# Dividing the attention output with channels on partitions, and four steps in another place

## The reference

```
x = x + attention(layernorm(x)) @ Wo.T       # 16 heads of 8 channels, 64-token window over
                                             # the token's block and the block before
n = layernorm(x)
scores = sigmoid(n @ gate_kernel) + gate_bias
comb   = the 4 best experts of the 2 best groups of 4, weights normalised, times 2.5
x = x + sum_e comb[e] * (silu(n @ w_gate[e]) * (n @ w_up[e])) @ w_down[e]      # 16 experts of 64
      + (silu(n @ sw_gate) * (n @ sw_up)) @ sw_down                            # shared, 128 wide
```

## Time and profile before

| | before |
|---|---|
| median of 3 runs (lowest to highest) | 708.99 us (707.56 to 709.0) |
| the profiled execution: time, span | 710.96 us, 709.2 us |
| mean granted clock of TensorE, of full speed | 0.984 |
| busy PE, PEld | 662.5 us (93%), 521.9 us (74%) |
| busy DVE, ACT, POOL | 590.6 (83%), 530.9 (75%), 478.5 us (67%) |

### The profile page before, as it was taken

How to read it: one execution, slowest core, us unless ns; L and a number is a source line. 1 busy time by engine, 2 the same in 40 slices (tenths; PEclk the granted TensorE clock), 3 DMA queues, 4 the chain that set the end, 5 groups by cost and what they waited for, 6 DMA issues and landing times.

```text
span 709.2 us, 20018 instructions
## 1 busy us (share of the span) xinstructions
PE 662.5 (93%) x6488; PEld 521.9 (74%) x6488; DVE 590.6 (83%) x1708; ACT 530.9 (75%) x1635; POOL 478.5 (67%) x599
## 2 busy tenths in 40 slices
PE   3988889999999999999999999999999999989996
PEld 2767657777787877778787877778787877767775
DVE  2777797989989898988989898998989898888663
ACT  3775869787887879787887879787887879763432
POOL 3503157878788787877778687877878686776523
PEclk9998899999999999999999999999999999999999
DMA  6000022040414123040413113040313213041321
GB/s 174 20 13 31 1 73 96 17 141 28 130 50 120 59 74 105 19 131 30 122 58 116 63 63 117 12 137 30 120 59 105 74 56 110 6 134 35 117 76 46
DMA packets 50245, 52.60 MB, mean 74 GB/s; under 512 B 5664, under 2 KB 31904, under 8 KB 50080
## 3 DMA queue, kind: packets, MB, share of 16 engines
q1 hardware_dynamic: 50208, 52.14, 23.7%
HBM read 43.20 MB, written 4.72 MB: 68 GB/s over the span
## 4 chain that ended last, share of the span: by engine, by line
PE 30%; ACT 28%; DVE 19%; issue 12%; POOL 8%; DMA 1%; DVEq 1%; POOLq 0%; ACTq 0%; SPq 0%
ACT probs L603 12%; DVE neg_max L778 6%; PE PS L1057 5%; PE PS L903 4%; ACT q_by_head L554 4%; PE PS L865 4%; PE PS L867 4%; PE PS L866 4%; ACT v_bd L554 3%; ACT th L570 3%; DVE tu L767 3%; DVE probsT L738 3%; POOL hh L482 2%; POOL X L539 2%; POOL X L533 2%
## 5 line engine op out<-in xcount | busy, mean ns | idle before, releaser
L603 ACT ACTIVATE probs<-PS,neg_max 128x96 f32<-128x96 f32 (+1 forms) x1024 | 247.8, 351 | 75.7 <-DVE neg_max L778 75.7
L477 POOL TENSOR_TENSOR gate<-gate,spread 128x512 f32<-128x512 f32 x124 | 158.7, 1280 | 105.5 <-ACT gate L554 53.1
L482 POOL TENSOR_TENSOR hh<-gate,tu 128x512 f32<-128x512 f32 x108 | 139.3, 1290 | 14.7 <-DVE tu L767 7.3
L1057 PE MATMUL PS<-wd,hh 128*128 128x128 f32 x1024 | 137.5, 277 | 7.7 <-DVE OUT L793 2.9
L1057 PEld LDWEIGHTS PS<-wd,hh 128*128 128x128 f32 x1024 | 126.8, 192 | 20.7 <-DVE OUT L793 9.8
L778 DVE TENSOR_REDUCE neg_max<-PS 128x4 f32<-128x384 f32 (+1 forms) x256 | 122.1, 516 | 13.4 <-PE PS L903 11.7
L767 DVE SCALAR_TENSOR_TENSOR tu<-th,PS 128x512 f32<-128x512 f32 x128 | 87.5, 684 | 51.3 <-ACT th L570 39.5
L865 PE MATMUL PS<-x_hi,w_hi 128*128 128x512 f32 x288 | 125.0, 434 | 0.0
L570 ACT ACTIVATE th<-PS 128x512 f32<-128x512 f32 x128 | 80.5, 629 | 50.9 <-PE PS L867 49.3
L738 DVE STREAM_TRANSPOSE probsT<-probs 128x768 f32<-128x768 f32 (+1 forms) x128 | 114.4, 894 | 0.0
L867 PE MATMUL PS<-x_lo,w_hi 128*128 128x512 f32 x288 | 114.2, 397 | 0.0
(11 more groups left out here) (108 smaller groups left out, 986.9 us busy)
## 6 DMA issues: line engine op xcount, KB each, us to landing
spread<-weights_by_expert SPq DMA_DIRECT2D x248, 128.0 KB, 3.0
X<-x SPq DMA_DIRECT2D x32, 256.0 KB, 3.4
OUT<-H SPq DMA_DIRECT2D x16, 256.0 KB, 3.0
out<-OUT SPq DMA_DIRECT2D x16, 256.0 KB, 3.0
ffn_stage<-w_gu SPq DMA_DIRECT2D x1, 1152.0 KB, 7.0
wd<-w_down SPq DMA_DIRECT2D x1, 512.0 KB, 6.8
weights_by_expert<-cT SPq DMA_DIRECT2D x16, 32.0 KB, 1.6
probsT<-w_att SPq DMA_DIRECT2D x1, 192.0 KB, 3.1
```

What stands on the lines that cost most here:

```text
L477: tt(gate2[:, :], gate[:, k % 2, :], spread[:, k % SP_BUFS, :], ALU.mult).then_inc(s_g2, 1)
L482: tt(hh[:, k % 2, :], gate2[:, :], tu[:, k % 2, :], ALU.mult).then_inc(s_h, 1)
L603: ins = nc.scalar.activation(probs[:, u % PROB_BUFS, tt, 2 * rows + e, j0:KW], PS[:, rows, n * KW + j0:n * KW + KW], ACT.Exp, bias=neg_max ...
L1057: ins = mm(PS[:, 7, r], hh[:, k % 2, r], wd[:, k, :], start=(k == 0 and n == 0), stop=(k == NP - 1), skip_group_check=True)
```

## The change

The division keeps channels on partitions. DVE takes the reciprocal of the 128x32 sums before turning them. POOL multiplies the turned reciprocals by a mask, so that `by_block` (128 x 256) holds for each of eight query blocks only the lanes of that block (`EXPAND`, stages 14 and 17, steps 6 and 1). At `OT` PE multiplies a constant 0/1 map `to_channel` with it in one f32 matmul, which puts each token's reciprocal on the partitions of its channels, and DVE multiplies `o_f` with the result into `oT`. `ON`, its transposes and ACT's copy to `oT` are gone. The next values matmuls wait for DVE's product in place of ACT's copy. The two maps are made once, by DVE and POOL.

Four things move: DVE's addition to `OUT` from the middle of step 5 to the end of step 4 (stage 36; SP's store goes with it); the shared expert's matmuls on PE ahead of the values matmuls of step 1, and `fa` on DVE ahead of the turning; the statistics of the first norm ahead of the turning in step 3; and the extra matmuls also run in steps 0 to 3 of slot 3 (`warming`).

```diff
-OT, ON, OW = 14, 15, 16
+EXPAND = (14, 17)
+OT, OW = 14, 16
...
-YE = 37
+YE = 36
...
-    (POST, (OT, OT + 4, ON, ON + 4, OW, OW + 4, SH)), (WEIGHTS, (CT,)))
+    (POST, (OT, OT + 4, OW, OW + 4, SH)), (WEIGHTS, (CT,)))
...
+def warming(slot, s):
+
+    return filling(slot) or slot.fixed and slot.n == 3 and s < FF % STEPS
...
-        o_rs = sb("o_rs", [P, 8, 4])
-        o_n = sb("o_n", [P, 2, P])
+        lane_of = sb("lane_of", [P, 4])
+        block_of = sb("block_of", [P, NQ])
+        to_channel = sb("to_channel", [P, P])
+        by_block = sb("by_block", [P, GB, NQ, Q])
...
-        sums_of = ident.rearrange("p (v h c a) -> p c h a v", v=4, h=2, c=4)
...
+                    for b, stage in enumerate(EXPAND):
+                        g, _ = at(sl, s, stage)
+                        if g:
+                            if not (g.fixed and g.n == 0):
+                                taken(pool, slot_before(sl), (OT + 4 * b) % STEPS, POST)
+                            pool.wait_ge(s_sum_t, g.n * GB + b + 1)
+                            whole = [P, NQ, Q]
+                            tt(by_block[:, b, :, :], sums_t[:, b, :].unsqueeze(1).broadcast_to(whole),
+                               block_of[:, :].unsqueeze(2).broadcast_to(whole), ALU.mult).then_inc(s_exp, 1)
                     if sl.fixed and sl.n == 0 and s == LN1 + 1:
                         pool.wait_ge(s_w, 16 * LOADS)
+                        pool.wait_ge(s_lane, 1)
+                        for a in range(4):
+                            shape = [P, 4, D]
+                            ins = tt(to_channel[:, 32 * a:32 * a + 32].rearrange("p (v d) -> p v d", d=D),
+                                     lane_of[:, a:a + 1].unsqueeze(2).broadcast_to(shape),
+                                     grouprow.unsqueeze(2).broadcast_to(shape), ALU.mult)
+                        ins.then_inc(s_chan, 1)
...
-                    g, b = at(sl, s, ON, 4, GB)
-                    if g:
-                        side, bank = filled(act, sl, s, POST)
-                        copy(oT[:, :], bank[:, 0:T]).then_inc(s_taken[side], 1)
...
+                        v_.tensor_reduce(block_of[:, :], ident.rearrange("p (v t a) -> p t v a", t=NQ, a=HG),
+                                         mybir.AxisListType.XY, ALU.add)
+                        v_.tensor_reduce(lane_of[:, :], ident.rearrange("p (x a) -> p a x", a=HG),
+                                         AX_X, ALU.add).then_inc(s_lane, 1)
...
                             if u % 4 == 3:
                                 dve.wait_ge(s_sum, g.n * NU + u + 1)
+                                link(sl, v_.reciprocal(sums[:, b, :], sums[:, b, :]))
                                 v_.transpose(sums_t[:, b, :], sums[:, b, :]).then_inc(s_sum_t, 1)
...
-                    g, _ = at(sl, s, YE)
-                    if g:
-                        dve.wait_ge(s_dn, g.n + 1)
-                        dve.wait_ge(s_cp[g.par], turn(g))
-                        v_.tensor_tensor(OUT[:, g.par, :, :], tiles(PS[:, 7, :]), OUT[:, g.par, :, :],
-                                         ALU.add).then_inc(s_y, 1)
                     if s == (RT + 1) % STEPS:
                         for place in range(2, 6):
                             routing(sl, s, place)
...
-                        link(sl, v_.reciprocal(o_rs[:, :, :], bank[:, T:T + Q].rearrange("p (a v) -> p a v", v=4)))
-                        v_.tensor_tensor(o_n[:, :, :].rearrange("p n (a v d) -> p (n a) v d", v=4, d=D),
-                                         bank[:, 0:T].rearrange("p (a v d) -> p a v d", v=4, d=D),
-                                         o_rs[:, :, :].unsqueeze(3).broadcast_to([P, 8, 4, D]),
-                                         ALU.mult).then_inc(s_taken[side], 1)
+                        dve.wait_ge(s_o, g.n * GB + b + 1)
+                        v_.tensor_tensor(oT[:, :], o_f[:, :], bank[:, 0:T], ALU.mult).then_inc(s_taken[side], 1)
...
-                    turn_probs()
+                    g, _ = at(sl, s, SH)
+                    if g:
+                        side, bank = filled(dve, sl, s, POST)
+                        dve.wait_ge(s_ths, g.n + 1)
+                        v_.scalar_tensor_tensor(fa[:, :], th_s[:, :], 1.0, bank, ALU.add, ALU.mult
+                                                ).then_inc(s_taken[side], 1)
                     g = first_norm(sl, s)
                     if g:
                         dve.wait_ge(s_x[g.par], turn(g))
                         stats(sl, X[:, g.par, :, :], NT, st1, mv1).then_inc(s_mv1, 1)
+                    turn_probs()
...
-                    g, _ = at(sl, s, SH)
-                    if g:
-                        side, bank = filled(dve, sl, s, POST)
-                        dve.wait_ge(s_ths, g.n + 1)
-                        v_.scalar_tensor_tensor(fa[:, :], th_s[:, :], 1.0, bank, ALU.add, ALU.mult
-                                                ).then_inc(s_taken[side], 1)
                     sum_probs()
+                    g, _ = at(sl, s, YE)
+                    if g:
+                        dve.wait_ge(s_dn, g.n + 1)
+                        dve.wait_ge(s_cp[g.par], turn(g))
+                        v_.tensor_tensor(OUT[:, g.par, :, :], tiles(PS[:, 7, :]), OUT[:, g.par, :, :],
+                                         ALU.add).then_inc(s_y, 1)
                     g, _ = at(sl, s, XT)
...
-                    if filling(sl) and at(sl, s, SC, 1, NU)[0]:
+                    if warming(sl, s) and at(sl, s, SC, 1, NU)[0]:
                         for _ in range(BUSY):
                             mm(PS[:, 7, 0:WV], w_hi[:, WQ:WQ + P], w_hi[:, WQ:WV], start=True, stop=True)
...
+                    g, _ = at(sl, s, SH)
+                    if g:
+                        x2 = x2_hi[:, g.par, :], x2_lo[:, g.par, :]
+                        pe.wait_ge(s_x2l, g.n * GB + GB)
+                        for place, n in ((POST, WG), (LATE, WU)):
+                            side, bank = free(place)
+                            exact3(bank, *w2(n + P * NP), *x2).then_inc(s_filled[side], 1)
+
...
                         if not later and not (g.fixed and g.n == 0 and b == 0):
-                            pe.wait_ge(s_o, g.n * GB + b)
+                            taken(pe, slot_before(sl) if b else sl, (OT if b else OT + 4) % STEPS, POST)
...
                         side, bank = free(POST)
-                        pe.wait_ge(s_o, g.n * GB + b + 1)
-                        for half in range(2):
-                            nc.tensor.transpose(bank[:, P * half:P * half + P], o_f[:, P * half:P * half + P], ident)
-                        pe.wait_ge(s_sum_t, g.n * GB + b + 1)
-                        for c in range(4):
-                            ins = mm(PS[32 * c:32 * c + 32, RING[side], T:T + Q], sums_t[:, b, :], sums_of[:, c, :, :, :],
-                                     start=True, stop=True)
-                        ins.then_inc(s_filled[side], 1)
-                    g, b = at(sl, s, ON, 4, GB)
+                        if g.fixed and g.n == 0:
+                            pe.wait_ge(s_chan, 1)
+                        pe.wait_ge(s_exp, g.n * GB + b + 1)
+                        mm(bank[:, 0:T], to_channel[:, :], by_block[:, b, :, :].rearrange("p t q -> p (t q)"),
+                           start=True, stop=True).then_inc(s_filled[side], 1)
+                    g, b = at(sl, s, OW, 4, GB)
                     if g:
                         side, bank = free(POST)
-                        taken(pe, sl, (s - 1) % STEPS, POST)
-                        for half in range(2):
-                            ins = nc.tensor.transpose(bank[:, P * half:P * half + P], o_n[:, half, :], ident)
-                        ins.then_inc(s_filled[side], 1)
-                    g, b = at(sl, s, OW, 4, GB)
-                    if g:
-                        side, bank = free(POST)
-                        taken(pe, slot_before(sl) if s == 0 else sl, (s - 1) % STEPS, POST)
+                        taken(pe, sl if b else slot_before(sl), (OT + 4 * b) % STEPS, POST)
                         if g.fixed and g.n == 0 and b == 0:
                             pe.wait_ge(s_wf, 16 * FFN_LOADS)
                         for half in range(2):
                             r = slice(P * half, P * half + P)
                             ins = mm(bank[:, r], oT[:, r], wo[:, :], start=True, stop=True)
                         ins.then_inc(s_filled[side], 1)
-                    g, _ = at(sl, s, SH)
-                    if g:
-                        x2 = x2_hi[:, g.par, :], x2_lo[:, g.par, :]
-                        pe.wait_ge(s_x2l, g.n * GB + GB)
-                        for place, n in ((POST, WG), (LATE, WU)):
-                            side, bank = free(place)
-                            exact3(bank, *w2(n + P * NP), *x2).then_inc(s_filled[side], 1)
-
```

(15 more changed lines are left out.)

## The result

| | before, same chip | after |
|---|---|---|
| median of 4 runs (lowest to highest) | 709.0 us (707.56 to 710.1) | 754.27 us (752.87 to 755.91) |
| ratio, with its 95% interval | 1 | 1.0632 [1.0604, 1.0661] |
| profiled execution: time, span | 710.96, 709.2 us | 752.87, 751.1 us |

The forecast was 687 us (679 to 698). The kernel became slower by 45.3 us, far outside the range and past the slower rival too (716).

A forecast was written before the change was run, and what follows sets the result against it. PE was taken to bound the slot; 1.4 us saved a slot, 16.8 over twelve, 20.9 with the other slots and drain, plus 1.6 for the fill, made 22.5 us off: 687 us forecast (679 to 698).

The forecast's parts named there:

- the slower rival: POOL's product releases PE in both halves and holds up PE and POOL work behind it; 716 us, chance 0.05.
- rival (3): The slower rival: POOL's product at 2.0 us loses 0.9 us a slot; 716 us, chance 0.05.
- The new wait for POOL's product: Step 6, PE at the new matmul: a new standstill of 0.4 us a slot, 0.3 in the sum.
- `ON`'s transposes: Two transposes of o_n per half group leave PE, saving 0.27 us each half, in steps 3 and 7.
- rival (1): ACT and DVE replace PE as the bound; the slot gains only 0.9 us; 696 us, chance 0.20.
- The shared products between scores and values: Shared products precede the values matmuls, which stand 1.4 us later; claimed free, as ACT copies o_f only afterwards.
- X: Step 4, PE's wait for POOL's normalisation: earlier statistics remove it, 0.45 us a slot.
- OUT: Step 5, PE's wait for DVE before the down products: the earlier addition removes it, 0.34 us a slot.
- fa: Step 2, PE's wait for DVE: fa ahead of the turning removes it, 0.27 us a slot.
- The matmul in place of the transposes: One f32 matmul of 256 columns per half, 0.46 us, replaces o_f transposes and spreading passes of 0.60 us.
- DVE's and ACT's chain: About as long as PE's from step 5 to 1; 0.2 us a slot taken off for DVE's longer chain and margin.
- The fill: Slot 3's warming matmuls keep PE's clock at 1.0: 1.6 us gained, best case 3.

The follow-up runs named there:

- after +19: The changed kernel with 19 more idle instructions (repeats of an already met wait) ahead of PE's first matmul; 699.6 us, ratio 0.9823 against before.
- the moves alone: The changed kernel with the old division and no warming in slot 3, leaving the moves of OUT, shared products with fa, and statistics; 702.27 us, ratio 0.9873.
- the late matmul: The changed kernel with 19 more instructions, the new matmul behind its step's down products and DVE's oT product at the step's end; 694.8 us, ratio 0.9763.
- the division alone: The changed kernel with 19 more instructions and the three moves undone, leaving new division and warming; 707.67 us, ratio 0.9973.

## Why the prediction was wrong

**The step that failed** is one that the prediction never took, a term of the sum put at nothing without a reason: it priced removed and added instructions by their time on the engine and let the place of PE's loop in its instructions be what it was. The unrolled slots 0 to 3 became 57 instructions shorter, the transposes and the spreading passes weighing more than the warming that was added; the loop slid from seven pieces into eight. That costs five times a standstill of 6.2 us and 2.9 us of half clock behind it, 45.5 us together; with 19 idle instructions the profiled execution is 53.3 us shorter (699.57 against 752.87). Of that, 50 are the five turns (89.0 against 39.5 twice, 10 us each: the 9.1 above and some 0.9 of work out of step behind them) and 3.3 the fill, which ended at 114.61 us in the one and 111.36 in the other: the clock was 0.50 from 64 to 68 us in the one and 1.00 in the other, a fall that comes and goes between executions, and I have one trace of each. No row that I cited could show the jump; the row of the instruction queue, 20 packets, and the loop's edges in the program, both within some 0.2 of a piece of a border (offset included), would have raised the question. The rivals had the right sign once, for another reason: POOL's product takes 0.62 us, not the 2.0 that rival (3) needed.

**The rest of the sum** (the row after +19): the slot gained 0.56 us by medians (0.50 over the whole loop) where 1.4 was forecast, and the kernel 12.6 us where 22.5 was. By the two profiled executions, 11.4 us apart, 5.9 came in the loop where 16.8 was forecast, 4.1 up to slot 4 where 3.4 was, and 1.4 behind the loop where 2.3 was.
- The new wait for POOL's product, taken at 0.4 us (0.3 in the sum), is 1.0 to 1.3 in the twelve slots, 1.13 at the median, and 19.1 us over 15 times. Step 6 is 0.88 longer than forecast. The product was sized rightly (0.62 us). That POOL would come 0.66 us earlier was not, since a transfer took part of the gain (0.33), nor that PE would come 0.79 earlier (1.10, mostly by the larger gain at X). This is the largest miss of the order of work. The same 0.61 us product at the other half, a step ahead, is waited for by nobody, as forecast.
- `ON`'s transposes: 0.27 forecast in step 3, got 0.0; in step 7, 0.20. In step 3 they filled time in which PE's next gate product waits for DVE anyway, as its weight load shows in the kernel with 19 more (before it had no such wait):

```profile
448.05 0.19 PEld L889 LDWEIGHTS PS<-x_hi,w_hi 128*128 128x128 f32 x1 [0.29 <-DVE tu L794]
```

  I counted all work taken off PE as won, although DVE's and ACT's chain was said to be as long as PE's there. It was rival (1) at one place of the slot.
- The shared products between scores and values: step 1 grew by 0.20 to 0.32 us in every kernel that has the move, and in none without it. I had counted it as free.
- X: 0.75 gained for 0.45. OUT: 0.43 for 0.34. These two and fa (0.43 in step 2 with the matmul's 0.14, forecast 0.41) stood as forecast or better, and the list of waits lost them all.
- The matmul in place of the transposes: 0.53 us from its start to the next work where nothing is waited for (441.60 to 442.13 in the kernel with 19 more), 0.60 before; forecast 0.46, so a half saved 0.07 there rather than 0.14.
- DVE's and ACT's chain: in the kernel with 19 more no step shows the 0.2 us that I took off for it. In the two where PE's own waits are gone from step 6, step 7 grew: to 4.99 us in the moves alone (before 4.62) and to 5.08 with the late matmul (from 4.42). In the moves alone PE then waits for the input that ACT copies:

```profile
468.86 1.04 PE L933 MATMUL PS<-ffn_stage,x_f 128*128 128x16 f32 x8 [0.15 <-ACT x_f L554]
```

  That is where the next bound seems to stand; with the late matmul some 0.3 of the 0.66 us are the shared bank's. No run takes the two apart.
- The fill: what the warming gives isn't settled. Slot 3 takes 38.33 us before. It takes 36.55 with warming and 19 more, and as little, 36.56, in the moves alone, which have no warming. But in the one pair that differs in the warming alone it takes 36.56 with it and 39.38 without. There the clock stayed at 1.00 from 68 us on with the warming (as forecast for slot 3), and without it fell to 0.62 and 0.52 from 76 to 84 us and to 0.83 and 0.74 from 88 to 96; yet slot 4 begins at the same time in both (114.6 and 114.4 us), since with the warming the clock had fallen in slot 2. In the kernel with 74 more it fell to 0.50 in spite of the warming. Each of these is one execution, so the 1.6 us of the sum are neither confirmed nor refuted.

The moves alone gained 0.47 us a slot and the division alone 0.06. Together they should give 0.5 and gave 0.56 (0.50 over the whole loop), with the wait that the moves lay bare; with the matmul out of the wait's way 1.07. Neither part alone shows how much that placement gives.

## What to carry to other kernels

Before a change to a long program with a loop, look at how many blocks of instructions the loop touches, and at the instruction queue's packets after each change: a count that grew by a multiple of the turns points to a loop that is fetched anew, and here a few idle instructions ahead of it, put where PE waits anyway, mended it. A change that is measured as a loss of some per cent is to be measured again with the loop held in place before it is judged. And where a wait is taken from an engine, follow it to its next transfer before its earlier time is passed on to what stands behind.

## What the hardware showed that I had not expected

- A loop of 1618 or 1702 instructions of PE is kept where it touches seven blocks of 256, and fetched anew, nine packets a turn, where it touches eight. The blocks count as if from 35 to 51 instructions ahead of the kernel's first: fitted to six kernels, and borne out by the one with 19 more, which counted from the first instruction would touch eight.
- The standstill at the jump was 2.3 to 6.4 us, by place. What sets the size isn't settled: 6.1 to 6.4 came where the loop, offset included, begins at most 17 instructions ahead of a border; the 2.3 to 3.9 at the other places follow no order that I see.
- A standstill of 2.3 to 2.9 us can bring the clock to 0.50, but doesn't always. Of the fifteen of that length twelve were followed by 0.50 and three (2.31, 2.41 and 2.83 us) by 1.00 throughout; all ten of 3.7 us and more were followed by 0.50. This is a window of the kernel with 227 more, just behind one of 2.43 us:

```profile
304.00:308.00 4.00, 4.00 (x14) 3.35 (x14) 0.00 (x0) 1.27 (x4) 0.00 (x0) 0.50 0.36 122
```

And this one of before with 109 more, behind one of 2.83 us (from 297.19 us on PE works again):

```profile
300.00:304.00 4.00, 3.96 (x57) 3.29 (x56) 2.89 (x6) 3.22 (x12) 3.48 (x6) 1.00 0.03 9
```

The refetch costs more than its standstill: 43 us between the kernels with 166 and 227 more, 12.3 of them the five standstills themselves and 5.0 the later start of slot 3 behind the longer padding. The rest is the half clock and work out of step behind it, which that pair doesn't take apart.
